# Explicit step lists for the fill and the drain of a software pipeline over 32 graphs

## The reference

```
x = layernorm(x + L0(x, a, adj, adj))        # A: pairwise score, normalised over all pairs, leaky relu,
                                             #    softmax over axis 1, weights @ x, sigmoid
x = layernorm(x + L1(x, adj, ...))           # B: h = x Wp + bp, masked softmax attention, (attn * adj) @ h,
                                             #    layernorm, relu;  C: adj @ h + (1+eps) h, W1, layernorm
                                             #    (Z), relu, W2, relu
x = layernorm(x + L2(x, adj, W, e, bias))    # D: softmax(edge table) split in diagonal and rest, two
                                             #    weights, bias
x = layernorm(x + L3(x, adj, W, src, dst))   # E: attention over neighbours, elu
```

## Time and profile before

| | |
|---|---|
| median of 3 runs | 1199.55 us |
| the profiled execution itself | 1201.41 us |
| its span, first to last instruction | 1199.5 us |
| PE busy | 1115.1 us (93%) |
| DVE busy | 1082.1 us (90%) |
| ACT busy | 1012.0 us (84%) |
| POOL busy | 405.5 us (34%) |

### The profile page before, as it was taken

One profiled execution on the slowest core, in us unless ns is written; L12 is line 12 of the kernel. 1 busy time (PEld: TensorE's weight loads), 2 busy tenths in 40 slices (PEclk: granted clock), 3 DMA queues, 4 the chain that ended last, 5 costly groups with the idle time before them and its releaser, 6 DMA issues.

```text
span 1199.5 us, 29294 instructions
## 1 busy us (share of the span) xinstructions
PE 1115.1 (93%) x7721; PEld 913.9 (76%) x7752; DVE 1082.1 (90%) x4214; ACT 1012.0 (84%) x2581; POOL 405.5 (34%) x800
## 2 busy tenths in 40 slices
PE   4778999999999999999999999999999999999864
PEld 3456788888777778888777788887777788878653
DVE  6898999999999999999999999999999999997542
ACT  3456799999999999999999999999999999998654
POOL 3122334423334344323433344233343443233211
PEclk9699999999999999999999999999999999999876
DMA  3000011011011111010011110110111100100000
GB/s 84 27 19 28 27 37 36 20 33 35 17 35 35 35 35 33 20 35 26 26 35 35 35 35 17 35 35 18 35 35 35 35 27 25 36 27 11 19 9 18
DMA packets 59459, 35.95 MB, mean 30 GB/s; under 512 B 3872, under 2 KB 54816, under 8 KB 59424
## 3 DMA queue, kind: packets, MB, share of 16 engines
q1 hardware_dynamic: 59424, 35.54, 9.7%
HBM read 18.75 MB, written 8.39 MB: 23 GB/s over the span
## 4 chain that ended last, share of the span: by engine, by line
DVE 46%; issue 28%; POOL 12%; PE 8%; ACT 2%; DVEq 2%; POOLq 0%; DMA 0%; ACTq 0%; SPq 0%
DVE wB L1116 5%; DVE pTB L1147 5%; DVE vA L1226 4%; DVE wE L1116 3%; DVE vA L1245 3%; DVE wE L1134 3%; POOL rirA L450 3%; POOL lnr_E L438 2%; POOL lnr_B L438 2%; DVE lnst_B L1268 2%; DVE lnst_D L1088 2%; DVE lnst_C L1088 2%; DVE t2B L1301 2%; DVE lnst_Z L1088 1%; DVE y_D L1318 1%
## 5 line engine op out<-in xcount | busy, mean ns | idle before, releaser
L750 PE MATMUL ps<-hE,pTE 128*128 128x128 f32 x1024 | 133.7, 279 | 0.1
L432 POOL TENSOR_TENSOR lnve_Z<-lnmv_Z,consts 128x4 f32<-128x4 f32 x32 | 17.1, 534 | 330.8 <-DVE lnmv_Z L1096 330.8
L678 PE MATMUL ps<-xsA,pA 128*128 128x128 f32 x1024 | 124.3, 281 | 1.2 <-ACT xsA L1555 1.2
L750 PE MATMUL ps<-hB,pTB 128*128 128x128 f32 x1024 | 124.9, 275 | 0.0
L750 PEld LDWEIGHTS ps<-hE,pTE 128*128 128x128 f32 x1024 | 122.8, 193 | 2.3 <-issue 0.6
L810 PE MATMUL ps<-att_j,xD 128*128 128x512 f32 x256 | 124.3, 609 | 0.0
L767 PE MATMUL ps<-gin_j,hgat 128*128 128x512 f32 x256 | 121.7, 599 | 0.0
L678 PEld LDWEIGHTS ps<-xsA,pA 128*128 128x128 f32 x1024 | 119.1, 195 | 1.5 <-ACT xsA L1555 1.3
L750 PEld LDWEIGHTS ps<-hB,pTB 128*128 128x128 f32 x1024 | 119.4, 192 | 0.2 <-issue 0.2
L1116 DVE SCALAR_TENSOR_TENSOR wE<-ps,hE,y2E 128x512 f32<-128x512 f32 x128 | 90.0, 745 | 24.8 <-ACT y2E L1577 21.5
L1545 ACT ACTIVATE pA<-vA,nmA,rirA 128x512 f32<-128x512 f32 x128 | 104.6, 818 | 4.7 <-DVE vA L1245 4.7
(11 more groups left out here) (237 smaller groups left out, 3040.9 us busy)
## 6 DMA issues: line engine op xcount, KB each, us to landing
xA<-in_x_dram SPq DMA_DIRECT2D x32, 256.0 KB, 2.6
xrA<-in_x_dram SPq DMA_DIRECT2D x32, 256.0 KB, 2.7
xrB<-xB SPq DMA_DIRECT2D x32, 256.0 KB, 2.2
out_dram<-xout SPq DMA_DIRECT2D x32, 256.0 KB, 2.2
adj_i<-in_adj_dram SPq DMA_DIRECT2D x1, 1024.0 KB, 5.2
a<-in_L_gnn_a_dram SPq DMA_DIRECT2D x2, 64.0 KB, 5.6
w_sb<-in_L_gnn_W_dram SPq DMA_DIRECT2D x2, 64.0 KB, 4.5
l2w<-in_L_gnn_W_dram SPq DMA_DIRECT2D x2, 64.0 KB, 3.7
```

Of the source, the lines that this page charges most:

```text
L678: last = mm(at("aggA")[:, i * P:(i + 1) * P], pA[:, j, i * P:(i + 1) * P], xsA[:, j], start=(j == 0), stop=(j == NT - 1))
L750: last = mm(at("agg" + n)[:, i * P:(i + 1) * P], att[n]["pT"][:, i, j], att[n]["h"][:, j, 0:P], start=(j == 0), stop=(j == NT - 1))
```

## The change

The one list per engine becomes three: `fill` (turns 0 to 6), `turn` (the loop body, turns 7 to 28), `drain` (turns 29 to 36). The loop body holds the same steps in the same order as before, without the steps of the setup; on DVE and ACT the delays are one higher and the loop starts one turn later, so it begins with the same graph. `fill` and `drain` name each step with its graph, `t.graph(GRAPHS - 3, norm_D, copy_xTE)`, and `t.once(...)` places the steps of the setup between them. So in these turns the order can differ from that of the loop. On PE a dictionary keeps which use stands in which bank while the lists are issued; the setup's uses have new banks. The counting signals of the setup (`SETUP`) follow the new order. The loop is opened with `hint_back_edge=True`.

```diff
-        def turns(eng, body):
-
-            for it in range(LAST_DELAY + 1):
-                body(Turn(it, GRAPHS))
-            with eng.Fori(LAST_DELAY + 1, GRAPHS) as it:
-                body(Turn(it, GRAPHS))
-            for it in range(GRAPHS, GRAPHS + LAST_DELAY):
-                body(Turn(it, GRAPHS))
+        def turns(eng, fill, turn, drain):
+
+            fill(Ramp({}))
+            with nc.Fori(FILL_TURNS, GRAPHS - DRAIN_TURNS, 1, engines=[eng.engine], hint_back_edge=True) as it:
+                turn(Turn(it))
+            last = {}
+            for bank, uses in enumerate(IN_BANK):
+                use, delay = uses[-1]
+                last[bank] = (use, GRAPHS - DRAIN_TURNS - 1 - delay)
+            drain(Ramp(last))
...
+            def fill(t):
+                t.graph(0, load_xA)
+                t.once(load_a, load_adj, load_weights)
+                t.graph(0, load_xrA)
...
+                t.graph(GRAPHS - 2, ax_D0)
+                t.graph(GRAPHS - 3, transpose_xE)
+                t.graph(GRAPHS - 2, scale_xD)
+                t.graph(GRAPHS - 3, h3_E, h012_E, t_E)
+                t.graph(GRAPHS - 2, ax_D1)
+                t.graph(GRAPHS - 1, gin0, gin1)
...
```

More of the change, by code:

```diff
@@ L38 @@
 B, E = "BE"
-LAST_DELAY = 5
+FILL_TURNS, DRAIN_TURNS = 7, 3
 BIG = 2.0 ** 100
@@ L47, with __init__, now, before @@
 class Graph:
-    def __init__(self, turn, delay):
-        self.turn, self.delay = turn, delay
-        self.g = turn.it - delay
-        self.real = not isinstance(turn.it, int) or 0 <= self.g < turn.graphs
-        self.now = turn.it - (delay - 1)
-        self.last = self.g
-        self.first = isinstance(turn.it, int) and self.g == 0
+    def __init__(self, turn, g, first=False):
+        self.turn, self.g, self.last, self.first = turn, g, g, first
+    @property
+    def now(self):
+        return self.g + 1
     def tile(self, j, tiles=4):
         return self.now if tiles == 1 else self.g * tiles + (j + 1)
-class Once:
-    def __init__(self, turn):
-        self.turn = turn
 class Turn:
-    def __init__(self, it, graphs):
-        self.it, self.graphs = it, graphs
-    def graph(self, delay):
-        return Graph(self, delay)
+    def __init__(self, it):
+        self.it = it
+    def before(self, delay):
+        return LoopGraph(self, delay)
     def run(self, step, delay):
-        g = self.graph(delay)
-        if g.real:
-            step(g)
-    def once(self, part, it):
-        if isinstance(self.it, int) and self.it == it:
-            part(Once(self))
+        step(LoopGraph(self, delay))
+class LoopGraph(Graph):
+    def __init__(self, turn, delay):
+        Graph.__init__(self, turn, turn.it - delay)
+        self.delay = delay
+    @property
+    def now(self):
+        return self.turn.it - (self.delay - 1)
+class Ramp:
+    def __init__(self, in_bank):
+        self.in_bank = in_bank
+    def graph(self, g, *steps):
+        for step in steps:
+            step(Graph(self, g, first=(g == 0)))
+    def once(self, *pieces):
+        for piece in pieces:
+            piece(Graph(self, 0))
 def resnorm_gnn(nc, x, adj, l0_a, wp, bp, a_src, a_dst, gat_g, gat_b, eps, w1, b1, mlp_g, mlp_b, w2, b2,
@@ L455, in turn @@
                 t.run(rstd_Z, 3)
-                t.once(numbers, 0)
-                t.once(no_edge_E, 4)
                 t.run(rstd_D, 4)
-                t.once(loops_E, 2)
                 t.run(rstd_C, 3)
@@ L902, in _ @@
+            turns(pe, fill, turn, drain)
         @block.vector
@@ L1449, in _ @@
+            turns(dve, fill, turn, drain)
         @block.scalar
@@ new lines, in turn @@
+            def turn(t):
+                t.run(copy_h012B, 3)
+                t.run(exp_A0, 2)
+                t.run(y2_B, 3)
+                t.run(exp_A1, 2)
+                t.run(copy_pE1, 6)
+                t.run(exp_A2, 2)
+                t.run(copy_pE2, 6)
+                t.run(norm_Z, 4)
+                t.run(copy_pE3, 6)
+                t.run(exp_B0, 3)
+                t.run(copy_zT, 4)
+                t.run(exp_B1, 3)
+                t.run(exp_B2, 3)
+                t.run(exp_A3, 2)
+                t.run(exp_B3, 3)
+                t.run(relu_E, 6)
+                t.run(expm_E, 6)
+                t.run(scale_xA, 2)
+                t.run(norm_D, 5)
+                t.run(norm_C, 4)
+                t.run(tanh_A, 2)
+                t.run(copy_xTE, 5)
+                t.run(norm_B, 3)
+                t.run(copy_h012E, 5)
+                t.run(copy_h3E, 5)
+                t.run(norm_E, 6)
+                t.run(y2_E, 5)
+                t.run(relu_B, 3)
+                t.run(copy_xTD, 4)
+                t.run(copy_rowsA, 1)
+                t.run(copy_axD, 4)
+                t.run(norm_A, 2)
+                t.run(exp_E0, 5)
+                t.run(copy_ginT, 3)
+                t.run(exp_E1, 5)
+                t.run(copy_xTB, 2)
+                t.run(copy_pE0, 5)
+                t.run(exp_E2, 5)
+                t.run(exp_E3, 5)
+                t.run(copy_h3B, 2)
@@ L1728 @@
+            turns(act, fill, turn, drain)
 _INS = ["x", "adj", "L0_gnn_a", "L1_gnn_Wp", "L1_gnn_bp", "L1_gnn_a_src", "L1_gnn_a_dst", "L1_gnn_gat_g",
```

1429 lines of the change are left out of this document (1203 added, 226 removed), and 14 rows, old and new, of the table IN_BANK.

## The result

The changed kernel takes 1195.11 us (median of 6 runs, 1194.19 to 1195.62), the kernel before 1199.95 us beside it (6 runs, 1198.19 to 1200.38): ratio 0.9959, 95% interval 0.9949 to 0.9969. So 4.8 us faster, where I predicted 12.0. The profiled execution has a span of 1193.3 us against 1199.5.

The account below looks back on a forecast made before the run. Steady turns have PE and DVE nearly full, so only fill and drain can shorten; the drain is latency-bound on three serial E stages. 3.0 + 3.5 + 0 + 5.5 = 12.0 us off 1199.55 gives 1187.5 us, range 1178 to 1198.

Parts of the forecast that it names:

- The start: First loads: a issued earlier, so DVE starts near 5.0 us and v_A0 near 17.9; 3.0 us, bounds 0 to 3.1.
- The rest of the fill: Setup turns before the loop: new order gives back part of DVE's idle time; 3.5 us, bounds 0 to 9.2.
- PE is no obstacle: In the fill: PE does not limit the gain on DVE, as it idles 22 us there.
- The loop: Loop body, 22 turns: same steps plus a hint; +0.5 us between -6.6 and +6.6, nothing together with the turns without a branch.
- a refetch of code: Rival at the loop's head: each turn stalls for code or hint; 1.0 us a turn would give 1209.5 us; chance 0.11.
- The four turns without a branch: Turns taken out of the loop: each saves at most 0.30 us, 1.2 us in all; 0.5 us taken.
- are PE-bound and give nothing: Turns 29 to 31, up to 1111 us: PE busy 35.83 of 36 us, so no gain.
- The drain's order: Last turns: new order shortens the chain of E stages; 5.5 us, bounds -1.5 to 12.0.
- the two periods that I priced: Drain, between the norm_D starts of graphs 29, 30 and 31: 4.2 us less in the first, 1.3 in the second.

Follow-up runs that it names:

- e10: Changed kernel with the load of adj, and the weight loads behind it, issued only once both halves of a have landed; 1192.84 us, 0.9931 of the kernel before.
- e3: Kernel before with only the changed kernel's drain list; old fill, no hint; 1193.48 us, 0.9951 of the kernel before.
- e11: Kernel before with the changed kernel's drain list and all turns written out without a loop; 1173.46 us, 0.9777 of the kernel before.
- e6: Changed kernel with no loop, its 22 turns written out in the loop's order; 1176.83 us, 0.9813 of the kernel before.
- e7: Changed kernel with rows_A of graph 2 moved on PE ahead of the first half of gin of graph 0; 1197.6 us, 0.9991 of the kernel before.
- e9: Changed kernel with SyncE's loads of the fill in the old order from the third graph on; 1194.73 us, 0.9953 of the kernel before.
- e14: Changed kernel with scale_xA of graph 4 moved ahead of relu_E and expm_E of graph 0 on ScalarE; 1195.37 us, 0.9952 of the kernel before.
- e8: Kernel before with the changed kernel's drain list and two turns in the loop body, no hint; 1224.03 us, 1.0201 of the kernel before.
- e1: Changed kernel without the prefetch hint on the loop's branch; 1195.72 us, 0.9961 of the kernel before.
- e13: Kernel before with xA and a loaded first and adj issued only once a has landed; 1202.78 us, 1.002 of the kernel before.

## Why the prediction was wrong

The direction was right, and 1195.11 lies in the range of 1178 to 1198, but the forecast of 1187.5 missed by 7.6 us. Three steps failed: the start and the rest of the fill, which together gave -3 us for the 6.5 forecast, and the price of a turn in the loop, whose miss of 3 us went the other way and hid part of the first two.

*The start* (3.0 expected): about nothing (`v_A0` at 20.53 to 21.44 us in executions of the new fill, 20.65 to 21.40 in those of the old). I took the 2.6 us of an undisturbed load for `a` and named as bound only that `adj` be late. That `adj` and the weights, issued right behind `a`, would slow it down stood nowhere: DVE's first instruction came at 7.30 us, not 5.0. In e10, where it can't, DVE starts at 5.13 and the changed kernel gains 3 us more.

*The rest of the fill* (3.5 expected, bounds 0 to 9.2): a loss of 3.0 us by the mean of the traces; by the ratios 1.0 us (e3 against the changed kernel) to 4.3 us (e11 against e6). This is the larger error, and it is in the bound. "By the time the loop is entered DVE has done the same work, so what the new order can give back is its idle time" allows only for gains; a new order can add idle time as well, and did: most of it (2.3 us) behind `v_A0` of graph 4, where DVE's dots of graph 5 wait 1.4 to 2.6 us for `xA` (0.3 to 1.2 in the old fill), PE behind them, and its clock falls in the worse executions. I also said that PE is no obstacle because it idles 22 us; it is one just because it idles, since what follows an idle stretch runs at the lower clock (e7). Which of the moved steps makes the loss is not settled: of three repairs e7 made it worse, e9 left it and e14 moved it to another wait.

*The loop* (0 expected): 34.06 against 34.03 us a turn, about 0.6 us over 18 turns. Right. Its rival, a refetch of code, did not come with a body of one turn; e8, with two turns and no hint, shows it at 2.9 us an iteration.

*The four turns without a branch* (0.5 expected, at most 1.2): three times the bound. I priced a branch by DVE's 0.30 us and the 0.2 us of the earlier trace rows; a turn written out saves 0.9 to 1.1 us. The largest part of it, DVE's wait of 0.59 us for `rirA` in every turn of the loop, stood in the waits of the kernel before (5.9 us in 340), and my price left it out. Turns 29 to 31, which "are PE-bound and give nothing", gave 3.6 us in this way.

*The drain's order* (5.5 expected): 4.3 us on the loop by the traces, 1 to 3 without one; by the two periods that I priced, 4.2 for graph 29 to 30, as predicted, and 4.2 in place of 1.3 for the next. There some luck is in it: the loop's order gave 25.7 to 27.6 us for that period in six executions (27.64 is the longest), the drain list 22.5 to 23.9 in fourteen. The mechanism of the first is as described (half product ahead of `xE`'s transposes, no idle PE, high clock). What I had not counted is that the stretch begins later: `norm_C` of graph 30 stands ahead of `norm_D` of graph 29 and waits 1.83 us for POOL, so `xE` comes 2.15 us later than before, though `y_E` in front of it only 1.20.

Summed over the traces: +3.0 for start and fill (`v_A0` of graph 5), +0.6 for the loop, -7.9 for the end, -4.3 us; measured -4.8.

The best version is e11, 0.9777 of the kernel before: the old fill, no loop, the drain list. The new fill with `adj` held back (e10) and no loop was not run.

## What to carry over

A loop can cost more than its branch: compare the period of the loop with that of the same steps written out before you price it, and compare the waits of the two, since the larger part here was no wait at the branch. The idle time of a stretch bounds what a new order can gain, not what it can lose: a reordered prologue can lengthen a wait of PE until its clock falls behind it (e1, e7). An order of loads and the order of the steps that use them are one change: the loads of e13 lost 2.4 us in the old lists and gained 3 us in the new ones (e10).
